# A graph layer pair on one core: the node starts counted on ScalarE, and each ranking call's last range finished in the next

## The reference

```
h = maximum(layernorm(x), 0)
x = x + gcn(gcn(h, W1, b1) with relu, W2, b2)
h = maximum(layernorm(x), 0)
msg = relu(concat(h[src], edge_attr) @ W1 + b1)
agg = segment_sum(msg, dst) / maximum(count, 1)
x = x + relu(concat(h, agg) @ W2 + b2)

gcn(x, W, b):  h = x @ W;  deg = 1 + edges into the node
               out = segment_sum((h[src], and h itself) / sqrt(deg[src] * deg[dst]), dst) + b
```

## Time and profile before

| | |
|---|---|
| median of 3 runs | 2926.35 us (2925.55 to 2926.58) |
| the profiled execution, its own time | 2923.46 us |
| its span, first to last instruction | 2921.6 us |
| TensorE busy in the span | 2554.8 us (87%) |
| GpSimd busy | 1842.2 us (63%) |
| VectorE busy | 1612.8 us (55%) |
| ScalarE busy | 1021.3 us (35%) |
| mean granted clock of TensorE | 0.954 of full speed |

### The profile page before, as it was taken

One profiled execution on the slowest core, in us unless ns is written; L12 is line 12 of the kernel. 1 busy time (PEld: TensorE's weight loads), 2 busy tenths in 40 slices (PEclk: granted clock), 3 DMA queues, 4 the chain that ended last, 5 costly groups with the idle time before them and its releaser, 6 DMA issues.

```text
span 2921.6 us, 53392 instructions
## 1 busy us (share of the span) xinstructions
PE 2554.8 (87%) x18818; PEld 2059.8 (71%) x18819; DVE 1612.8 (55%) x3028; ACT 1021.3 (35%) x2891; POOL 1842.2 (63%) x1747
## 2 busy tenths in 40 slices
PE   1756578999999995999996599999999999999997
PEld 0104357888778894888885487877878777777786
DVE  7889897888766556000002654544545455454556
ACT  6504133566667764000000233333333333333331
POOL 2852363677887771756661277777777777777750
PEclk9997699999999997989998699999999999999999
DMA  9102221332434442746563222232222232222321
GB/s 372 37 6 74 77 63 59 133 124 106 150 116 153 177 180 89 237 155 239 210 231 113 89 76 79 76 90 77 79 76 80 79 88 79 76 79 76 90 49 48
DMA packets 111653, 327.75 MB, mean 112 GB/s; under 512 B 33282, under 2 KB 71527, under 8 KB 104855
## 3 DMA queue, kind: packets, MB, share of 16 engines
q10 hardware_dynamic: 6624, 147.72, 12.6%
q0 software_dynamic: 58352, 93.38, 12.4%
q1 hardware_dynamic: 46377, 82.75, 8.1%
HBM read 197.11 MB, written 126.61 MB: 111 GB/s over the span
## 4 chain that ended last, share of the span: by engine, by line
PE 71%; DVE 18%; issue 5%; POOL 2%; ACT 2%; DMA 1%; DVEq 1%; ACTq 0%; SPq 0%; POOLq 0%
PE ps_feat L889 12%; PE ps_node L889 12%; PE ps_extra L1036 7%; PE ps_sum L997 7%; PE ps_pre L990 6%; DVE region_c L1680 4%; DVE region_c L1676 4%; PE ps_node L1020 3%; PE ps_node L1024 3%; PE ps_pre L877 3%; PE ps_sum L1020 2%; PE ps_feat L1020 2%; PE ps_sum L1024 2%; PE ps_feat L1024 2%; PE ps_turn L1012 2%
## 5 line engine op out<-in xcount | busy, mean ns | idle before, releaser
L630 POOL DMA_INDIRECT rows<-table,region_a x928 | 895.6, 965 | 384.7 <-issue 262.4
L648 POOL DMA_INDIRECT permuted<-edge_rows_of,slot_of_edge x640 | 728.1, 1138 | 323.0 <-issue 150.6
L889 PE MATMUL ps_node<-region_a,region_b 128*128 128x256 bf16 x3528 | 450.5, 273 | 1.8 <-ACT region_b L1126 1.8
L1849 DVE TENSOR_SCALAR region_b<-ps_turn,consts 128x512 f32<-128x512 f32 (+1 forms) x280 | 191.6, 684 | 461.8 <-PE ps_turn L1012 418.4
L889 PE MATMUL ps_feat<-region_a,region_b 128*128 128x256 bf16 x3528 | 445.8, 273 | 0.0
L889 PEld LDWEIGHTS ps_node<-region_a,region_b 128*128 128x128 bf16 x3528 | 341.4, 97 | 45.4 <-ACT region_b L1126 2.0
L889 PEld LDWEIGHTS ps_feat<-region_a,region_b 128*128 128x128 bf16 x3528 | 342.3, 98 | 44.1
L1680 DVE TENSOR_TENSOR region_c<-iota_key,region_c 128x1568 bf16<-128x1568 f16 (+1 forms) x324 | 354.1, 1093 | 0.0
L1676 DVE TENSOR_TENSOR region_c<-iota_units,region_c 128x1024 bf16<-128x1024 bf16 x324 | 224.3, 692 | 136.5 <-PE ps_turn L877 91.3
L1164 ACT ACTIVATE region_a<-ps_pre 128x392 bf16<-128x392 f32 x384 | 190.8, 497 | 215.8 <-PE ps_pre L877 207.9
L1036 PE MATMUL ps_extra<-region_b 128*128 128x128 f32 x1960 | 265.2, 275 | 0.0
(11 more groups left out here) (255 smaller groups left out, 3747.1 us busy)
## 6 DMA issues: line engine op xcount, KB each, us to landing
counts<-region_a ACTq DMA_DIRECT2D x24, 3136.0 KB
region_a<-counts ACTq DMA_DIRECT2D x22, 3136.0 KB
permuted<-region_b SPq DMA_DIRECT2D x21, 833.0 KB, 23.6
region_a<-permuted SPq DMA_DIRECT2D x20, 833.0 KB, 4.7
region_a<-attr_t_in SPq DMA_DIRECT2D x58, 256.0 KB
rows<-table,region_a POOLq DMA_INDIRECT x928
edge_rows_of<-edge_cols_in POOLq DMA_DIRECT2D x20, 544.0 KB
permuted<-edge_rows_of,slot_of_edge POOLq DMA_INDIRECT x640
```

The lines of the kernel that those rows point to most:

```text
L630: nc.gpsimd.indirect_dma_start(rows[:, s, j * D:(j + 1) * D], None, tables[2], bass.IndirectOffsetOnAxis(ap=message_rows[:, c * TC + j:c * ...
L648: nc.gpsimd.indirect_dma_start(permuted, bass.IndirectOffsetOnAxis(ap=slot_of_edge[:, r * RT + k:r * RT + k + 1], axis=0), edge_rows_of[:, ...
L889: ins = mm(strip_bank(buf), parts[:, h, k], counts[buf][:, h], start=(h == 0 and k == 0), stop=(h == SB - 1 and k == PARTS - 1), skip_grou ...
L1849: v.tensor_scalar(source_hot[u % 2][:, 0:n], ps_turn[:, 0:n], partition, None, ALU.is_equal).then_inc(B["source"], 1)
```

## The change

It does five things.

- `RANKS_BEFORE_STARTS` is 14: the four searches are followed by 3, 4, 3 and 4 ranges instead of 3 each, and 6 ranges are left for behind the starts instead of 8.
- `rank_edges` finishes range r-1 behind the one-hot and scan of range r in every case, so the last range of a call is finished in the next call. `ranks_taken(RANGES - 1)` finishes the last of all.
- The comparison and sum on VectorE are gone. ScalarE, behind its 49 search activations, runs 49 activations over 128 columns: Sign of (`node_half` minus target), summed into `starts[:, 2]`. That sum is the number below less the number not below, so half of it plus 64 is the count; the 64 (P / 2) goes into the step that makes 128 times the tile number, and one VectorE step combines both.
- `node_tiles_gathered` is two semaphores, one for the first three searches (36 blocks) and one for the fourth (13). ScalarE starts on the first 36 when all 36 have landed.
- `edge_w_loaded` and `message_rows_loaded` become one, `message_inputs_loaded`, for which TensorE and GpSimd both wait at five transfers.

```diff
-RANKS_BEFORE_STARTS = 12
+RANKS_BEFORE_STARTS = 14
...
-                pool.wait_ge(message_rows_loaded, 16)
+                pool.wait_ge(message_inputs_loaded, 16 * (TC + 1))
...
-                            bass.IndirectOffsetOnAxis(ap=tile_of_i[:, b:b + 1], axis=0)).then_inc(node_tiles_gathered, 16)
+                            bass.IndirectOffsetOnAxis(ap=tile_of_i[:, b:b + 1], axis=0)).then_inc(node_tiles_gathered[q // 3], 16)
...
-            pe.wait_ge(edge_w_loaded, 16 * TC)
+            pe.wait_ge(message_inputs_loaded, 16 * (TC + 1))
...
+                for q, blocks in enumerate(SEARCHES):
+                    act.wait_ge(node_tiles_gathered[q // 3], 16 * (len(blocks) if q == 3 else SEARCHES[2][-1] + 1))
+                    for b in blocks:
+                        nc.scalar.activation(node_tiles[:, b], node_tiles[:, b].bitcast(I32), ACT.Sign, bias=node_half[:, b:b + 1], scale=-1.0,
+                                             accum_out=starts[:, 2, b:b + 1]).then_inc(searched, 1)
...
+            def ranks_taken(r):
+                take_ranks(r)
+                if r % RANK_BATCH == RANK_BATCH - 1:
+                    slots_of(r)
+
             def rank_edges(ranges):
-                hot_blocks(ranges[0])
-                blocks_upto(ranges[0])
                 for r in ranges:
-                    if r + 1 in ranges:
-                        hot_blocks(r + 1)
-                        blocks_upto(r + 1)
-                    take_ranks(r)
-                    if r % RANK_BATCH == RANK_BATCH - 1:
-                        slots_of(r)
+                    hot_blocks(r)
+                    blocks_upto(r)
+                    if r:
+                        ranks_taken(r - 1)
...
-                v.tensor_scalar(starts[:, 1, 0:SB], tile_of[:], float(P), None, ALU.mult)
-                dve.wait_ge(node_tiles_gathered, 16 * SB)
-                v.tensor_tensor(node_tiles, node_tiles.bitcast(I32), node_half.unsqueeze(2).to_broadcast([P, SB, P]), ALU.is_lt)
+                v.tensor_scalar(starts[:, 1, 0:SB], tile_of[:], float(P), P / 2, ALU.mult, ALU.add)
                 dve.drain()
-                v.tensor_reduce(starts[:, 2, 0:SB], node_tiles, AX.X, ALU.add)
-                dve.drain()
-                v.tensor_tensor(starts[:, 0, 0:SB], starts[:, 1, 0:SB], starts[:, 2, 0:SB], ALU.add).then_inc(starts_ready, 1)
+                dve.wait_ge(searched, 2 * SB)
+                v.scalar_tensor_tensor(out=starts[:, 0, 0:SB], in0=starts[:, 2, 0:SB], scalar=0.5, in1=starts[:, 1, 0:SB],
+                                       op0=ALU.mult, op1=ALU.add).then_inc(starts_ready, 1)
...
             rank_edges(range(RANKS_BEFORE_STARTS + 2, RANGES))
+            ranks_taken(RANGES - 1)
```

More of the change, by code:

```diff
@@ L304, in build @@
         setup_ready = sem("setup_ready")
-        edge_w_loaded = sem("edge_w_loaded")
+        message_inputs_loaded = sem("message_inputs_loaded")
         rows_loaded = sem("rows_loaded")
         x_loaded = sem("x_loaded")
-        message_rows_loaded = sem("message_rows_loaded")
         rows_reduced = sem("rows_reduced")
@@ L316, in build @@
         tiles_found = sem("tiles_found")
-        node_tiles_gathered = sem("node_tiles_gathered")
+        node_tiles_gathered = [sem(f"node_tiles_gathered_{j}") for j in range(2)]
         per_node_ready = sem("per_node_ready")
@@ L471, in _ @@
             for j in range(TC):
-                sp.dma_start(edge_w[DE * j:DE * (j + 1), j, :], t["L1_gnn_W1"][D:D + DE, :]).then_inc(edge_w_loaded, 16)
+                sp.dma_start(edge_w[DE * j:DE * (j + 1), j, :], t["L1_gnn_W1"][D:D + DE, :]).then_inc(message_inputs_loaded, 16)
             sp.wait_ge(starts_int, 1)
@@ L577, in _ @@
             sp.dma_start(h2, t["x_nodes"].rearrange("p b d -> p (b d)")).then_inc(x_loaded, 16)
-            sp.dma_start(message_rows, t["src_t"][:, DT:NT]).then_inc(message_rows_loaded, 16)
+            sp.dma_start(message_rows, t["src_t"][:, DT:NT]).then_inc(message_inputs_loaded, 16)
             store_table(2)
```

## The result

The changed kernel takes **2899.73 us** (median of 4 runs, 2896.85 to 2901.91) against 2925.95 of the kernel before (4 runs): ratio 0.9911, 95% interval [0.9894, 0.9928]. The profiled execution took 2901.68 us (span 2899.9, clock 0.955), 21.8 less than the one before.

A forecast was written before the change was run, and what follows sets the result against it. The setup was taken as bound by GpSimd's gathers, then VectorE's two long passes, then its ranking. 5.65 - 6.6 - 13.75, with rounding -14.8 us, gave 2911.5 us from a median of 2926.35; range 2905 to 2920.

The forecast's parts named there:

- The end of the gathers: Setup, GpSimd's node gathers: 14 ranges beside them at 2.82 us each, so they end 5.65 us later, landed at 159.25.
- The rival on this point: GpSimd becomes the setup's bound, ranges up to 4.40 us: gain 9 to 11, 2915 to 2917; 0.12 with the stalls-only-moved rival.
- the bounds I gave (2.65 to 4.40): Limits in us on what one range's ranking costs GpSimd's gathers; the upper is its whole one-hot and scan.
- The count: Setup, ScalarE's 49 activations replacing VectorE's compare and sum: pitch 0.52 us, 7.1 us on the path instead of 13.74, 6.6 less.
- The ranking after the starts: VectorE, end of setup: 6 ranges instead of 8, none a call's end, 34.45 us instead of 48.2, 13.75 less.
- The cover of the visit gathers: GpSimd's 21 visit-start gathers beside 6 scans land at some 212.2, VectorE comes at 215.5: 3.3 us of cover.
- Semaphores: TensorE's wait for edge weights now also holds for the message rows, both asked for long before: costed at nothing.
- clock: TensorE's clock falls from 1.00 to 0.50 by 260 us; a shift was costed at nothing, 3 us either way allowed.
- shift of what follows: Work from 231 us on is kept as it is, so what the setup's end gains moves all that follows.
- Rivals 2 (slow activations): ScalarE's count: gain gone at pitch 0.94 us, 0.2% slower from 1.06, 2965 at 1.73; chance 0.03 for slower.
- 3 (gain absorbed): Something fixed in time after 231 us absorbs the gain, 2926 as before; 0.06 together with a slow-activation pitch of 0.85 to 1.05.
- 4 (stalls only moved): VectorE's ranking: the deferral only moves stalls if TensorE falls behind; 10 us won, 2916; 0.12 with the GpSimd-bound rival.

The follow-up runs named there:

- psum_scan: The changed kernel with the scan's first input in PSUM instead of SBUF and the scan in four pieces; 2898.41 us, ratio 0.9907 to the kernel before.
- act_waits: The changed kernel with each of the 49 counting activations also waiting for the one ahead of it; 2902.19 us, ratio 0.992 to the kernel before.
- after_again: The changed kernel unaltered, measured again on another chip against the kernel before; 2902.38 us against 2925.11, ratio 0.9919.
- no_scalar_2: The changed kernel with the count on VectorE and the two old semaphores, repeated on another chip; 2935.51 us, ratio 1.0035 to the kernel before.
- split_scan: The changed kernel with the scan in the same four pieces but its first input left in SBUF; 2897.12 us, ratio 0.9902 to the kernel before.

## Why the prediction was right or wrong

**The end of the gathers: wrong, by 6.2 us (the last landed at 153.10, forecast 159.25).** The step that failed is "the other 33.9 us fall to the 12 ranges ranked beside them: 2.82 each". It took a mean over two kinds of ranges as a price. The rows had both kinds: 62.65 with 3.98 in the earlier trace rows, in the scan of a close pair, and scans 6.21 apart in the earlier trace rows. The ends of the calls, which I had counted as VectorE's loss alone, were GpSimd's too: each call began with a close pair of scans. With the deferral one such pair is left of four, and the mean was 2.38. This step and the pitch below make up the setup's 7.9 us beyond the forecast (22.7 for 14.8); 22.7 us alone would have put the time at 2903.7, below the range, and a gain of 18 us and more had been given a chance of 0.02. The rival on this point went the wrong way: GpSimd did stay the bound, but its price fell. Beside rows that show two spacings I should have asked what the change does to the spacing; the bounds I gave (2.65 to 4.40) did not hold what came.

The Trainium skill, "SBUF — State Buffer", "Who interferes with whom", was right in kind: a VectorE instruction with two SBUF inputs holds GpSimd off for as long as it runs, and psum_scan agrees (0.94 us beside a scan of 3.57 with one input in PSUM). What I made of it, up to 4.40 us a range, was wrong, since only gathers that start within such a step pay, and each to some 0.8 us behind its end.

**The count: mechanism right, size off by 1.8 us.** The failing term is "the pitch is 0.40 + 0.12 = 0.52 us". The 0.40 was right (0.39 to 0.40 measured); the 0.12 was a wait on a semaphore, which act_waits gives back (0.53). My lower bound, 0.43, lay above the 0.387 measured, since I had allowed no overlap of one activation with the next. The first 36 were hidden as forecast. The Trainium skill, "ScalarE: Activation LUTs", "Rules for kernel authors", names relu, max, min, add and mul as work for VectorE and not ScalarE; stretched to this compare and sum, that rule would have left it on VectorE. The work did get longer, 49 × 0.387 = 19.0 us for 13.4; it gained since all but 5.0 us lay beside the gathers.

**The ranking after the starts: right.** From the one-hot at 159.17 to the last scan at 193.59 it took 34.42 us, forecast 34.45; the last range's stall stayed (203.07), the other ends of calls have no stall. `per_node` did not wait.

**The cover of the visit gathers: held, and wider.** The last was issued at 200.57 and had landed some 2.6 us later (the median of the late ones); VectorE came for them at 207.62, 4.4 us behind that where 3.3 were forecast. The six scans beside them cost 2.45 us each instead of 2.65, for the same reason as in the first point.

**Semaphores, clock, shift of what follows: as forecast.** The setup's 22.7 us is in full in after_again's time. No run takes the merged semaphore alone. The clock's share, allowed with 3 us either way, is no larger than the spread. Rivals 2 (slow activations), 3 (gain absorbed) and 4 (stalls only moved) did not come about. But that a kernel can lose 26 us behind a better setup (no_scalar_2: 14.2 gained there, 12.1 lost in all), with the same code there, was in no rival: no_scalar_2 is the absorbed gain, by a cause that stays open, and that the change was spared it is luck.

## What to carry to other kernels

Where two engines hold each other off, the price of a step isn't its mean: lay the two timelines over each other, find the rule for one transfer (here: what starts in a two-input step ends some 0.8 us behind it), and ask how the change moves the spacing. When two edits act on one chain, price them together: deferral and more ranges were worth 3.8 and 1.1 us alone and 14.2 as a pair. Once the hold is gone, look for the next wait: some 70% of what split_scan and psum_scan spared GpSimd became waiting for tiles. And when a later stage with unchanged code moves by a per cent, pad the program with idle instructions, beside the unpadded one on the same chip, before believing any story about the edit.

## What was unexpected of the hardware

- A gather in a scan with two SBUF inputs takes up to 4.02 us, in one with an input in PSUM 0.94 to 0.99.
- A stage of the program ran 1199 to 1236 us with the same instructions; a kernel with 16 one-column memsets on VectorE some 1.7 ms ahead of its start had a ratio 0.6% lower than one with idle activations on the same chip, and 0.8 to 1.2% lower than the unpadded one on others.
- Two chips took 3468 and 3514 us for the kernel that takes 2925 on the others, at a mean granted clock of 0.90 instead of 0.954; the setup is as long on them, and what lies behind it some 20 to 22% longer. A clock 5% lower doesn't make that up, and no run shows what does.
